# A routed feed-forward kernel behind attention: attention sums, score blocks and the third batch's routing steps in another order

## What is computed

```python
x = x + attn(layernorm(x))      # scores = (x*w_lhs)(x*w_rhs)^T, softmax over the row, times x
x = x + ffn(layernorm(x))       # each row goes to its 2 best of 8 experts (128 -> 512 -> 128, gelu)
```

## Time and profile before

| | |
|---|---|
| median of 3 runs | 305.31 us |
| the profiled execution | 305.57 us, of which 304.0 us is the span from the first instruction to the last |
| busy share of the span | PE 89%, DVE 75%, ACT 65%, POOL 59% |
| the chain that ended last | PE 50%, POOL 14%, issue 13%, DVE 9%, DMA 7%, ACT 5% |
| granted TensorE clock | 0.976 on average; 0.9 or more in every slice up to the last two |

### The profile page before, as it was taken

How to read it: one execution, slowest core, us unless ns; L and a number is a source line. 1 busy time by engine, 2 the same in 40 slices (tenths; PEclk the granted TensorE clock), 3 DMA queues, 4 the chain that set the end, 5 groups by cost and what they waited for, 6 DMA issues and landing times.

```text
span 304.0 us, 8244 instructions
## 1 busy us (share of the span) xinstructions
PE 269.3 (89%) x2223; PEld 240.0 (79%) x2223; DVE 229.5 (75%) x1002; ACT 196.4 (65%) x427; POOL 180.6 (59%) x245
## 2 busy tenths in 40 slices
PE   7999999899999988899999699998999999999400
PEld 3589998789978977678888589987999999998400
DVE  4699898979878868988989777794565556666736
ACT  2447378897359772545679947774788788898200
POOL 8111036017667792687877657777777777777600
PEclk9999999999999999999999999999999999999955
DMA  6960000000401100111251143124233332221986
GB/s 195 412 293 4 0 3 0 3 0 0 144 27 57 37 27 11 37 45 38 69 140 63 38 118 109 55 73 125 73 97 100 95 93 82 81 73 55 352 279 248
DMA packets 15450, 28.51 MB, mean 94 GB/s; under 512 B 3904, under 2 KB 9920, under 8 KB 15152
## 3 DMA queue, kind: packets, MB, share of 16 engines
q1 hardware_dynamic: 10224, 16.88, 17.0%
q0 software_dynamic: 4608, 10.07, 9.9%
q10 hardware_dynamic: 576, 1.05, 1.0%
HBM read 15.83 MB, written 12.16 MB: 92 GB/s over the span
## 4 chain that ended last, share of the span: by engine, by line
PE 50%; POOL 14%; issue 13%; DVE 9%; DMA 7%; ACT 5%; SPq 1%; POOLq 0%; DVEq 0%; ACTq 0%
PE av_ps L1387 15%; PE av_ps L1182 11%; POOL slots L846 10%; PE sc_ps L1366 4%; PE sc_ps L1368 3%; PE sc_ps L1367 3%; DVE neg_piece L1503 3%; DMA raw_proj<-results 3%; DMA slots<-stage,slot 2%; DMA slots_in<-slots 2%; PE bank L1353 2%; PE sc_ps L1171 2%; PE bank L1158 1%; ACT h_all L972 1%; PE bank L1160 1%
## 5 line engine op out<-in xcount | busy, mean ns | idle before, releaser
L1094 ACT ACTIVATE raw_fc<-sc_ps,bfc,scale_down 128x128 f32<-128x128 f32 (+1 forms) x188 | 81.6, 530 | 0.7 <-PE sc_ps L1368 0.7
L950 POOL DMA_INDIRECT results<-prob,result_row x71 | 68.6, 967 | 22.1 <-issue 12.2
L846 POOL DMA_INDIRECT slots<-stage,slot x64 | 64.1, 1002 | 29.2 <-issue 18.9
L1387 PE MATMUL av_ps<-raw_proj,raw_fc 128*128 x568 | 72.7, 278 | 2.8 <-issue 1.9
L1182 PE MATMUL av_ps<-h_all,prob 128*128 128x137 f32 x512 | 73.2, 285 | 0.6 <-DVE lg_part L1534 0.4
L1387 PEld LDWEIGHTS av_ps<-raw_proj,raw_fc 128*128 128x128 f32 x568 | 67.0, 192 | 4.9 <-issue 4.5
L1182 PEld LDWEIGHTS av_ps<-h_all,prob 128*128 128x128 f32 x512 | 66.8, 190 | 4.4 <-DVE res L1531 1.6
L1366 PE MATMUL sc_ps<-h_all,wfc_hi 128*128 128x128 f16 (+1 forms) x188 | 43.2, 247 | 1.3 <-ACT raw_fc L1094 1.2
L1872 DVE TENSOR_TENSOR h_all<-av_ps,bpr 128x256 f32<-128x256 f32 (+1 forms) x47 | 16.9, 359 | 35.4 <-PE sc_ps L1368 31.8
L1368 PE MATMUL sc_ps<-h_all,wfc_lo 128*128 128x128 f16 (+1 forms) x188 | 43.1, 246 | 0.0
L1367 PE MATMUL sc_ps<-h_all,wfc_hi 128*128 128x128 f16 (+1 forms) x188 | 43.1, 246 | 0.0
(11 more groups left out here) (201 smaller groups left out, 523.4 us busy)
## 6 DMA issues: line engine op xcount, KB each, us to landing
slots_in<-slots SPq DMA_DIRECT2D x24, 132.0 KB, 2.2
raw_fc<-in_w_fc_dram SPq DMA_DIRECT2D x1, 2048.0 KB, 11.3
raw_proj<-in_w_proj_dram SPq DMA_DIRECT2D x1, 2048.0 KB, 15.5
res<-in_x_dram SPq DMA_DIRECT2D x3, 512.0 KB, 5.9
slots_in<-slots SPq DMA_DIRECT2D x23, 66.0 KB, 1.8
results<-prob,result_row POOLq DMA_INDIRECT x71, 2.3
slots<-raw_fc POOLq DMA_DIRECT2D x2, 528.0 KB, 4.1
slots<-stage,slot POOLq DMA_INDIRECT x64
```

What stands on the lines that cost most here:

```text
L846: pool.indirect_dma_start(out=slots[:, :], out_offset=bass.IndirectOffsetOnAxis(ap=slot[:, n, k:k + 1], axis=0), in_=stage[:, b % 2, t, :] ...
L950: pool.indirect_dma_start(out=results[:, :], out_offset=bass.IndirectOffsetOnAxis(ap=result_row[a][:, h:h + 1], axis=0), in_=gated[a][h], ...
L1094: ins = act.activation(hid[:, a % NH, c, 0:halves_of(k) * P], up_ps(k, c), ACT.Gelu_apprx_tanh, bias=bfc[:, e, c:c + 1], scale=scale_down[ ...
L1387: mm = pe.matmul(o, hid[:, a % NH, c, rows], wpr[:, e, c, :], start=(c == 0 and h == 0), stop=(c == HC - 1), skip_group_check=True)
```

## The change

PE, in every batch: `attend(b - 1, 14)` leaves its place between `score(b, 4)` and `score(b, 5)` and stands behind `score(b, 7)`, right before `attend(b - 1, 15)`. `score(b, 9)` stands before `shift_scores(1)` and its wait for maximum 8, where it stood behind it. ACT, in the third batch (b = 2, `B - 2`) only: the four `make_h2(3, t)` and `high_h2(3)` go from behind the exponentials 6 and 7, ahead of `keep_rows(5)`, to ahead of the exponentials 10 and 11. DVE, at the end of the third batch only: `find_slots(1)` and `add_logits(4)` go ahead of `low_parts(7)`; `keep_hrw(3)` goes ahead of `take_stats2(4)`, and `split_h2(3)` behind both.

```diff
-                    if n >= BT - 2 and b >= 1:
+                    if n >= BT - 2 and b >= 1 and b != B - 2:
                         for t in (0, 1) if n == BT - 2 else (2, 3):
                             make_h2(2 * b - 1, t)
                         if n == BT - 1:
                             high_h2(2 * b - 1)
                 keep_rows(2 * b + 1)
                 for n in range(BT, EXPS):
+                    if n in (BT + 2, BT + 3) and b == B - 2:
+                        for t in (0, 1) if n == BT + 2 else (2, 3):
+                            make_h2(2 * b - 1, t)
+                        if n == BT + 3:
+                            high_h2(2 * b - 1)
...
                 score(b, 4)
-                if b >= 1:
-                    attend(b - 1, 14)
                 pe.wait_ge(again_kept, TU * b + 1)
                 score(b, 5)
...
                 score(b, 7)
                 if b >= 1:
+                    attend(b - 1, 14)
                     attend(b - 1, 15)
...
                 shift_scores(0)
+                score(b, 9)
                 pe.wait_ge(max_made, maxed_at(b, 8))
                 shift_scores(1)
-                score(b, 9)
                 shift_scores(2)
...
+                if b == B - 2:
+                    find_slots(b - 1)
+                    add_logits(2 * b)
                 if b == 0:
                     take_stats(5)
                 if b + 1 < B:
                     low_parts(2 * b + 3)
                 if b == 0:
                     find_scales()
-                if b == B - 2:
-                    split_h2(2 * b - 1)
-                if 1 <= b < B - 1:
+                if 1 <= b < B - 2:
                     find_slots(b - 1)
                 if b + 1 < B:
 
-                    add_logits(2 * b)
+                    if b != B - 2:
+                        add_logits(2 * b)
                     if b == B - 2:
                         early = picks(ROUNDS_BY[b] - 2)
                         steps(early, 6)
                     row_max(b + 1, 0)
-                    take_stats2(2 * b)
+                    if b != B - 2:
+                        take_stats2(2 * b)
                     keep_hrw(b + 1)
+                    if b == B - 2:
+                        take_stats2(2 * b)
+                        split_h2(2 * b - 1)
```

## The result

The changed kernel takes 303.88 us, the median of 20 runs; the kernel before, run beside it as often, takes 305.58. The ratio is 0.9947, interval 0.9929 to 0.9965. The change gains 1.6 to 1.7 us, where 4.6 were forecast, and the time lies just above the forecast's upper end of 303.6. The profiled execution took 304.85, its span is 303.3. The busy shares are nearly those of before (PE 90%, DVE 76%, ACT 64%, POOL 59%), but the granted clock is 0.960 on average in place of 0.976.

What follows compares the result with a forecast made beforehand. PE sets the pace with DVE close behind, and POOL's scatters form a second path that must also come earlier. Gains of 0.2 + 1.2 + 1.2 + 1.3 + 0.7 = 4.6 take 305.57 to 301.0 us, range 300.0 to 303.6.

Steps and rivals of the forecast that it cites:

- Attend 14: PE, attend 14 behind score 7: the transpose of the maxima starts earlier, gain 0.6 in second and third batch each.
- Score 9: PE, score 9 ahead of shift 1 covers maximum 8: gain 0.6 in second and third batch each, 0.2 in the first.
- The rival that DVE takes over: PE's gain at shift 2 is lost, only DVE's own 2.7 counts: 302.9 us; chance 0.22.
- ACT in the third batch: Norm-tile block moved behind the row copy: shift 8 gains 1.2, 0.8 given back at attends 10 and 11, net 0.4.
- DVE at the end of the third batch: Places and logits fill DVE's wait for ACT's high parts at no cost; fourth batch's transpose comes 1.3 earlier.
- laid it on the scatters: Rival, POOL's chain grows: shared ports lengthen 20 scatters by 0.19 each, 3.8 of 4.6 lost, 304.8 us; chance 0.09.
- The fourth batch: Score 9 fills PE's wait at maximum 8, shift 2 comes 0.8 earlier, DVE takes over most: gain 0.7.
- POOL's wait of 0.76: Before half batch 6's second norm at 155.03: slack letting POOL, 3.9 earlier, start that norm up to 4.7 earlier.
- The sum: PE and DVE at 155: 0.2 + 1.2 + 1.2 + 1.3 + 0.7 = 4.6; both paths and tile 16 move by it.
- The third rival: ACT's moved block costs more than its wait, all 2.3 landing on PE in the third batch: 306.9 us; chance 0.05.

Runs made afterwards that it cites:

- e10: Second run of e8's kernel, unchanged: the changed kernel with POOL's third-batch weight subtractions and gate powers two scatters earlier; 300.7 us, ratio 0.9848.
- e5: Changed kernel with POOL writing zeros in place of the three weight subtractions in the third batch, low parts left out; 300.52 us, ratio 0.9853.
- e6: The changed kernel once more, unaltered, profiled a second time, as partner of the run with PE's wait filled; 303.33 us, ratio 0.9955.
- e8: Changed kernel with POOL's three weight subtractions and gate powers of the third batch two scatters earlier, nothing left out; 302.04 us, ratio 0.988.
- e9: e8's kernel with ACT's block (four norm tiles and their copy) back ahead of the copy of the row maxima; 301.99 us, ratio 0.9883.
- e2: Kernel before with PE's two moves alone, ACT's and DVE's programs as before; 303.27 us, ratio 0.9953.

## Why the prediction was wrong, step by step

**Attend 14** was right: forecast 0.6 in each of two batches, shown 0.67. **Score 9** was right by the trace, though no run took it back alone: from shift 0 to shift 2 PE now takes 1.26 (55.02 to 56.28) where it took 1.83. The rival that DVE takes over is out, for no wait stands at attend 0 or shift 3, and shift 2 of the second batch comes the full 1.41 earlier.

**ACT in the third batch** was right as a sum. Shift 8 comes 1.29 after its transpose, as forecast, and from shift 8 to the first score of the fourth batch PE takes 7.02 (104.01 to 111.03) where it took 6.18 in the trace of before, so 0.84 is given back; forecast 0.8. That it hit so closely is partly luck: the forecast's own times have each exponential at most 0.4 late, and the 0.8 was picked between 0 and 2.3. But the terms don't stand alone. The forecast gave PE's two moves 1.2 in the third batch and ACT's 0.4; taken away by itself ACT's move costs 1.5, and PE's moves by themselves brought 1.36 at POOL's norm (121.01) where 2.6 would be their sum. Whoever comes first at shift 8 waits for the other.

**DVE at the end of the third batch** is the step that failed, in the sentence "they cost nothing as long as ACT's parts come no earlier than 113.9". I took the 1.9 of places and logits from rows in which POOL stood idle and moved them beside POOL's subtractions (3.38 at 110.26 in the trace of before, a row that I didn't weigh). The forecast had put this term at nothing. Places and logits took 4.57 (109.30 to 113.87), where in `e10` they take 1.83. Of the 2.74 more, 0.56 to 0.58 was wait for ACT, as `e5` and `e10` show, and 2.15 came late at `low_parts(7)` (113.87 against 111.72). At POOL's second norm the same 2.2 stand between the changed kernel (153.04, second profile) and `e10` (150.81). The medians differ by 1.3 to 3.2 us; the intervals of `e6` and `e10` don't touch.

I had the rule for it, and laid it on the scatters. Of what moved, only the split has two SBUF inputs; the four statistics, which I counted too, have one (`stats<-res`). The scatters didn't grow: those between the norms took 0.95 to 1.08 in the changed kernel and in `e10`, but for the last, which took 1.38 or 1.39 and did so before the change too. One of before's was longer, 1.25 at 135.72, beside the split at 135.44, and is 0.96 now; the last, at 152.89, stands beside the split at 152.75. I had looked past both rows when I wrote that none shows a scatter held up. The rest of this step holds: with the pair free, POOL's norm of half batch 4 comes 3.90 earlier (118.47 against 122.37), and the forecast was 3.9.

**The fourth batch** was forecast to give 0.7 and gave it at first: in `e10` shift 2 comes 4.60 earlier than before (126.65 against 131.25). The ranks on DVE come 4.39 earlier and the norm of half batch 6 only 4.22. So 0.3 is kept, and POOL's wait of 0.76 before that norm stays as it was in every kernel, where the forecast used it up. The rows show why it stays. One small operation of the table, `reach<-reach` at L597, takes 0.25 before and 0.36 in `e10`, where the one just before it (L594, the same shape) takes 0.17 in both; beside it runs a scatter of POOL. DVE and POOL before, then in `e10`:

```profile
148.52 0.25 DVE L597 TENSOR_SCALAR reach<-reach 128x8 f32<-128x8 f32 x1
147.84 0.96 POOL L846 DMA_INDIRECT slots<-stage,slot  x1 [0.30 <-issue]
```
```profile
144.20 0.36 DVE L597 TENSOR_SCALAR reach<-reach 128x8 f32<-128x8 f32 x1
143.62 0.96 POOL L846 DMA_INDIRECT slots<-stage,slot  x1 [0.30 <-issue]
```

In all 13 traces this operation ends 0.02 to 0.03 before that scatter does, and POOL's norm of half batch 6 starts 6.25 to 6.27 after its end. So by the rows DVE follows POOL's chain here, and what the forecast took for two paths with a slack of 0.76 between them is one: POOL's 3.9 of the norm before, and the 0.3 of the one shorter scatter. No run moved the operation or the scatter, so that the one holds the other is read and not tried.

**The sum** was 4.6; with the pair free `e8` and `e10` gained 3.7 and 4.6 by their ratios (2.9 and 4.5 by their medians) and `e5` 4.5 (4.2). Less the 2.2 of the hold-up and the 0.4 of the fourth batch it is 2.0, which is what POOL's second norm shows in the second profile of the changed kernel (153.04 against 155.03). By the ratios the changed kernel gained 1.6 and 1.4, with intervals up to 2.2 and 2.0. Whether the rest is chance or the clock stays open: within the changed kernel the executions with a low clock are the slow ones (in `e6` 305.47 and 304.96 at 0.957 and 0.958, 302.73 and 302.30 at 0.974 and 0.975), yet filling PE's wait got only 0.2 back, less than the runs can tell.

The third rival, that ACT's block costs more than its wait, is out by `e9`: without its move the kernel is slower.

## What to carry to other kernels

A step that is moved into a wait of its engine comes to stand beside other work of the other engines. Look up what they do in that stretch, and above all POOL's arithmetic on large tiles in SBUF, for every moved DVE operation with both inputs in SBUF. An idle stretch beside such arithmetic can be filled at its usual price by operations with one input in PSUM, as the rows of before show; and often it is easier to move POOL's arithmetic, which had time, than DVE's.

Gains of moves that meet at one wait can be forecast as a sum and not one by one.

A wait between two paths is slack only if nothing ties them on the way. One that stays the same to a hundredth in every version, as POOL's 0.76 here, asks for a look at where one engine follows the other.

## What the runs showed of the hardware

**The hold outlasts one instruction.** POOL's three subtractions of 128x512 take 1.13 each. The product that started 0.44 after the first of them got its turn only when all three were done, in two profiles (3.17 and 3.15 for the pair) and, from another starting point, in a third (2.10). The page of the Trainium skill named above speaks of the whole instruction; by that the pair would have been held some 0.7 (an estimate from the row: to the end of the first subtraction at 109.99), nearly all of which the wait of 0.57 would have hidden. The trace shows a hold over three instructions, with no turn for DVE between them. Not all POOL work holds such a product: beside three zero writes (1.44 in all, `e5`) the pair took 0.36, and in `e10` it took 0.35 at 109.31 beside the powers of the gates, which read 128x8 from SBUF and run from 108.02 for 1.67. So that POOL reads SBUF isn't enough by itself; what in the subtractions makes the difference, their size or their kind, no run tells. And a scatter seems to hold a DVE operation only towards its end: at L594 (143.99 in `e10`, 0.37 after the scatter began) it took its usual 0.17, and at L597, 0.58 after the scatter began, it was held to the scatter's end.

**The clock after a wait.** In the first profile of the changed kernel PE waited 1.78 and its clock read 0.54 in the next 5 us; in the second it waited 1.75 at the same place and the clock read 0.70. Microsecond by microsecond it reads 0.50 from 116 to 122 in the first and from 117 to 120 in the second. At tile 16 it read 0.76 for 7 us behind a wait of 2.23 (`e2`), and 1.00 behind one of 1.67 (`e5`). So nearly the same wait cost 1.4 us more in one execution than in the other (the router's products at 119.18 and 117.79), and one profile doesn't tell what the median has; the mean clock of every execution tells more. With the wait filled by three more scores the clock stayed at 1.00 from 105 to 130 and the median stayed where it was.
